# A decoder layer on one core: norms of six experts' weights taken during the recurrence, from staged copies

## The reference

```python
# 1. over 128 time steps, batch 16: an SSM state of 64 and a GRU state of 128
h_ssm = silu(h_ssm @ A.T + bxt);  r, z = sigmoid(i_r + h_r), sigmoid(i_z + h_z)
n = tanh(i_n + r * h_n);  h_rnn = (1 - z) * n + z * h_rnn
fused = g0 * (h_ssm @ Cw.T + Cb + dxt) + g1 * (h_rnn @ proj_w.T + proj_b)
# 2. retention over the context (per batch entry, decay mask, xpos)
out = ((q @ k.T) * mask) @ v
# 3. mixture of experts: 8 experts, top 2 of 8, capacity 320 tokens each
h = relu(xin @ w1[e] + b1[e]);  out = h @ w2[e] + b2[e]      # w1 256x1024, w2 1024x256
```

## Time and profile before

| what | value |
|---|---|
| runs without a profile | 504.99, 505.45, 508.36 us (median 505.45) |
| the profiled execution | 511.01 us, of which 509.2 us is the span of its instructions |
| busy share of the span | PE 80%, DVE 75%, ACT 46%, POOL 27% |
| granted TensorE clock, mean | 0.899 of full |
| HBM read, written | 35.04 MB, 11.01 MB |

### The profile page before, as it was taken

One profiled execution on the slowest core, in us unless ns is written; L12 is line 12 of the kernel. 1 busy time (PEld: TensorE's weight loads), 2 busy tenths in 40 slices (PEclk: granted clock), 3 DMA queues, 4 the chain that ended last, 5 costly groups with the idle time before them and its releaser, 6 DMA issues.

```text
span 509.2 us, 13431 instructions
## 1 busy us (share of the span) xinstructions
PE 405.5 (80%) x4676; PEld 312.4 (61%) x4676; DVE 382.2 (75%) x1575; ACT 235.2 (46%) x802; POOL 138.6 (27%) x207
## 2 busy tenths in 40 slices
PE   3979889899998999999999676217999999998000
PEld 3535667687786878778777565214677777776000
DVE  4477878987869879797867837686798888894184
ACT  0455265433233333333323224323988888963053
POOL 0013323211212112131201311044135554313384
PEclk9989989999799999999959789556999999999655
DMA  7970119020110201111011000006435656101482
GB/s 249 307 254 1 33 32 321 13 63 3 32 51 1 81 0 37 45 31 51 0 35 41 23 1 21 24 11 210 151 122 167 211 201 204 43 13 48 130 290 103
DMA packets 38238, 46.49 MB, mean 91 GB/s; under 512 B 4283, under 2 KB 32702, under 8 KB 38202
## 3 DMA queue, kind: packets, MB, share of 16 engines
q1 hardware_dynamic: 35002, 36.62, 22.2%
q0 software_dynamic: 3200, 9.40, 5.8%
HBM read 35.04 MB, written 11.01 MB: 90 GB/s over the span
## 4 chain that ended last, share of the span: by engine, by line
PE 45%; DVE 28%; issue 10%; ACT 9%; DMA 4%; POOL 3%; SPq 0%; ACTq 0%; DVEq 0%; POOLq 0%
PE bank L756 43%; DVE h L1123 3%; DVE mb L1114 3%; DVE ub L1112 3%; ACT arena L674 2%; DVE h L1126 2%; DVE hist L1124 2%; DMA wbuf<-in_w 2%; ACT arena L665 1%; DVE st L1186 1%; DVE vp L1460 1%; DVE tm L1155 1%; DVE mb L1115 1%; PE bank L1037 1%; ACT rzb L550 1%
## 5 line engine op out<-in xcount | busy, mean ns | idle before, releaser
L550 ACT ACTIVATE rzb<-bank 128x32 f32<-128x32 f32 x128 | 25.4, 198 | 99.3 <-PE bank L756 98.2
L756 PE MATMUL bank<-h,whp 128*128 128x32 f16 x1152 | 62.8, 185 | 5.1 <-DVE h L1123 2.6
L1112 DVE TENSOR_TENSOR_SCAN ub<-rzb,bank 128x32 f32<-128x32 f32 x128 | 27.9, 218 | 50.1 <-ACT rzb L550 49.1
L756 PE MATMUL bank<-arena 128*128 128x320 f16 x384 | 56.0, 304 | 1.4 <-DVE arena L1507 1.4
L756 PE MATMUL bank<-arena,kp 128*128 128x320 f16 x384 | 54.5, 299 | 0.0
L756 PEld LDWEIGHTS bank<-h,whp 128*128 128x128 f16 x1152 | 42.3, 97 | 15.4 <-DVE h L1126 3.5
L553 ACT ACTIVATE nb<-ub 128x16 f32<-128x16 f32 x128 | 27.9, 218 | 47.2 <-DVE ub L1112 47.2
L756 PEld LDWEIGHTS bank<-arena 128*128 128x128 f16 x384 | 37.7, 100 | 16.4 <-DVE arena L1507 1.6
L756 PEld LDWEIGHTS bank<-hsb,at_w 66*64 66x64 f32 x256 | 25.9, 140 | 34.7 <-DVE hsb L1118 22.5
L756 PEld LDWEIGHTS bank<-arena,kp 128*128 128x128 f16 x384 | 37.3, 98 | 14.1
L756 PE MATMUL bank<-hsb,at_w 66*64 66x16 f32 x256 | 37.3, 222 | 7.1 <-DVE hsb L1118 6.9
(11 more groups left out here) (206 smaller groups left out, 936.3 us busy)
## 6 DMA issues: line engine op xcount, KB each, us to landing
wbuf<-in_w SPq DMA_DIRECT2D x16, 1024.0 KB, 6.1
ybuf<-zero POOLq DMA_DIRECT2D x8, 512.0 KB, 7.4
wbuf<-ybuf SPq DMA_DIRECT2D x16, 256.0 KB, 5.6
xin_t<-in_xT SPq DMA_DIRECT2D x16, 128.0 KB, 2.3
arena<-in_ctxT SPq DMA_DIRECT2D x4, 512.0 KB, 7.5
xfin_t<-in_xT SPq DMA_DIRECT2D x16, 128.0 KB, 2.2
xres<-in_xtok SPq DMA_DIRECT2D x16, 128.0 KB, 2.1
x_d<-x SPq DMA_DIRECT2D x8, 256.0 KB, 2.3
```

What stands on the lines that cost most here:

```text
L550: nc.scalar.activation(od(rzb[:]), RZ[j][:, s * 2 * B:(s + 1) * 2 * B], ACT.Sigmoid).then_inc(q["r_ready"], 1)
L756: return nc.tensor.matmul(out_, lhsT, rhs, start=start, stop=stop, skip_group_check=True)
L1112: nc.vector.tensor_tensor_scan(ub[:], rzb[:, 0:2 * B], NS[j][:, s * 32:s * 32 + 32], 0.0, ALU.mult, ALU.add).then_inc(q["npre_ready"], 1)
```

## The change

The scales of all eight experts are made at once, ahead of the expert stage. For experts 2 to 7, iteration g of the recurrence squares expert g: `w1[g]` and `w2[g]` (1 MB each) are loaded to two stages in `arena[0]`, and ACT squares one piece of 128x512 of them after each of the steps 3, 4, 5, 8 (first layer), 9, 10, 12, 15 (second layer), and `b1[g]` after the last. SP asks for the next expert's first layer once ACT has squared the fourth piece, and for its second layer once it has squared the eighth; both requests stand inside `inputs(g)`. Those of expert 2 are asked for together in `inputs(1)`. Experts 0 and 1 are squared from `wbuf` as before. One matmul of 80 columns, one reduction, one power (16 elements per partition on POOL) and one set of scales serve all experts; `norms` and `scales` leave the expert loops of PE, DVE and POOL, and `squares` that of ACT. The weights are loaded a second time for the expert stage as before, so 12 MB are read twice. The diff, cut to its core (declarations, the changes of indices and the end of `squares` are left out):

```diff
+SQ_STEP = (3, 4, 5, 8, 9, 10, 12, 15)
+SQ_N = 5
...
+        b1s = sb("b1s", [P, E * FK])
+        wsum2 = sb("wsum2", [P, 2, E, SQ_N])
...
+        stage = [view(arena[0], 0, 4, 512), view(arena[0], 2048, 4, 512)]
+        wjunk = [arena3[:, 1536:2048].bitcast(BF16), arena3[:, 1024:1536].bitcast(BF16)]
...
+            def stage_1(g):
+                sp.dma_start(stage[0].rearrange("p a b -> p (a b)").rearrange("p (h f) -> p h f", h=HD), w1_d[:, g]).then_inc(q["wst0"], 16)
+
+            def stage_2(g):
+                sp.dma_start(stage[1].rearrange("p a b -> p (a b)").rearrange("p (k d) -> p k d", k=FK), w2_d[:, g]).then_inc(q["wst1"], 16)
+
             def inputs(g):
                 load_in(2 * g + 2, 0)
+                if not isinstance(g, int):
+                    sp.wait_ge(q["stq_ready"], 9 * (g - 2) + 5)
+                    stage_1(g + 1)
+                elif g == 1:
+                    sp.wait_ge(q["v_mm"], B)
+                    sp.wait_ge(q["csqs"], HD * B)
+                    stage_1(2)
+                    stage_2(2)
                 load_fin(2 * g + 2, 0)
+                if not isinstance(g, int):
+                    sp.wait_ge(q["stq_ready"], 9 * (g - 2) + 9)
+                    stage_2(g + 1)
                 load_in(2 * g + 3, 1)
                 load_fin(2 * g + 3, 1)
...
-            def norms(e):
-                pool.wait_ge(q["wnrm_ready"], 2 * e + 2)
-                pool.tensor_tensor(winv[e % 2][:], wnrm[e % 2][:], mhalf[:, 0:2], ALU.pow).then_inc(q["winv_ready"], 1)
-
-            norms(0)
+            pool.wait_ge(q["wnrm_ready"], 2)
+            pool.tensor_tensor(winv[:], wnrm[:], mhalf[:], ALU.pow).then_inc(q["winv_ready"], 1)
...
-                if e + 1 < E:
-                    norms(e + 1)
...
+            def stage_square(g, p):
+
+                if p % 4 == 0:
+                    act.wait_ge(q[f"wst{p // 4}"], 16 * (g - 1))
+                act.wait_ge(q["stq_ready"], 9 * (g - 2) + max(p, 1))
+                nc.scalar.activation(wjunk[p % 2][:, 0:512], stage[p // 4][:, p % 4, :], ACT.Square,
+                                     accum_out=wsum2[:, p // 4, bass.ds(g, 1), p % 4]).then_inc(q["stq_ready"], 1)
+                if p == 7:
+                    act.wait_ge(q["stq_ready"], 9 * (g - 2) + 8)
+                    nc.scalar.activation(wjunk[0][:, 0:FK], b1t[:, bass.ds(g * FK, FK)], ACT.Square,
+                                         accum_out=wsum2[:, 0, bass.ds(g, 1), 4]).then_inc(q["stq_ready"], 1)
+
             def iteration(g, A, M):
                 for s in range(CH):
                     rec(g, s // ST, s % ST)
+                    if M and s in SQ_STEP:
+                        stage_square(g, SQ_STEP.index(s))
...
+            def w_high(e, j, p, i):
+                if p % 2 == 0:
+                    act.wait_ge(q[f"w{p // 2 + 1}l{j}"], 16 * i + 16)
                 nc.scalar.activation(quarter(w1p[j][0], w2p[j][0], p), quarter(w1t[j], w2t[j], p), ACT.Copy,
-                                     scale=wscl[j][:, p // 2:p // 2 + 1]).then_inc(q["w_hi"], 1)
+                                     scale=wscl[:, bass.ds(p // 2 * E + e, 1)]).then_inc(q["w_hi"], 1)
...
+            squares(0)
             exponentials(1, TILES - 4, TILES)
-            squares(1, 1, 0)
+            squares(1)
+            act.wait_ge(q["wscl_ready"], 4)
...
-                if not (isinstance(e, int) and e >= E - 2):
-                    squares(e + 2, j, i + 1)
...
-            def norms(e, j, bk=1):
-                pe.wait_ge(q["wsq_ready"], 5 * e + 5)
-                mm(bank[bk][:, 384:390], ones[:], wsum2[j][:].rearrange("p w k -> p (w k)")).then_inc(q["wnsum"], 1)
-
-            norms(0, 0, 6)
+            pe.wait_ge(q["wsq_ready"], 10)
+            mm(bank[6][:, 384:384 + 2 * E * SQ_N], ones[:], wsum2[:].rearrange("p w e k -> p (w e k)")).then_inc(q["wnsum"], 1)
...
-                if not (isinstance(e, int) and e == 0):
-                    pe.wait_ge(q["wnrm_ready"], 2 * e + 1)
...
-                    if f == 1 and not last_:
-                        if not (first or isinstance(e, int) and e < 2):
-                            pe.wait_ge(q["yt_ready"], 2 * e - 2)
-                        norms(e + 1, 1 - j)
...
+            def norms():
+                dve.wait_ge(q["wnsum"], 1)
+                nc.vector.tensor_reduce(wtot[:], bank[6][:, 384:384 + 2 * E * SQ_N].rearrange("p (n k) -> p n k", k=SQ_N),
+                                        AX.X, ALU.add).then_inc(q["wnrm_ready"], 1)
+                dve.wait_ge(q["wnrm_ready"], 1)
+                nc.vector.tensor_scalar(wnrm[:], wtot[:], TINY, None, ALU.max).then_inc(q["wnrm_ready"], 1)
+
+            def scales():
+                dve.wait_ge(q["winv_ready"], 1)
+                nc.vector.tensor_scalar(wscl[:], winv[:], W_UP, None, ALU.mult).then_inc(q["wscl_ready"], 1)
+                dve.wait_ge(q["wscl_ready"], 1)
+                nc.vector.tensor_tensor(b1s[:].rearrange("p (e f) -> p e f", e=E), b1t[:].rearrange("p (e f) -> p e f", e=E),
+                                        wscl[:, 0:E].unsqueeze(2).to_broadcast([P, E, FK]), ALU.mult).then_inc(q["wscl_ready"], 1)
+                nc.vector.tensor_tensor(wprod[:], wscl[:, 0:E], wscl[:, E:2 * E], ALU.mult).then_inc(q["wscl_ready"], 1)
+                dve.wait_ge(q["wscl_ready"], 3)
+                nc.vector.reciprocal(wund[:], wprod[:]).then_inc(q["wscl_ready"], 1)
...
-                    if f == 1 and not last:
-                        norms(e + 1, 1 - j)
...
-                    if f == 4 and not last:
-                        scales(e + 1, 1 - j)
```

More of the change, by code:

```diff
@@ L112, in mk_decoder_kernel @@
         ones = sb("ones", [P, P])
-        mhalf = sb("mhalf", [P, 4])
+        mhalf = sb("mhalf", [P, 2 * E])
         epst = sb("epst", [P, 2])
@@ L215, in mk_decoder_kernel @@
         w2p = [[w[:, HD * FF:].rearrange("p (k d) -> p k d", k=FK) for w in ws] for ws in wparts]
[L216 to L225, removed]
+        b1s = sb("b1s", [P, E * FK])
+        wsum2 = sb("wsum2", [P, 2, E, SQ_N])
+        wtot = sb("wtot", [P, 2 * E])
+        wnrm = sb("wnrm", [P, 2 * E])
+        winv = sb("winv", [P, 2 * E])
+        wscl = sb("wscl", [P, 2 * E])
+        wprod = sb("wprod", [P, E])
+        wund = sb("wund", [P, E])
+        stage = [view(arena[0], 0, 4, 512), view(arena[0], 2048, 4, 512)]
+        wjunk = [arena3[:, 1536:2048].bitcast(BF16), arena3[:, 1024:1536].bitcast(BF16)]
         hp = [arena[0][:, i * FK * CAP // 2:(i + 1) * FK * CAP // 2].bitcast(F16).rearrange("p (f c) -> p f c", f=FK) for i in range(2)]
@@ L462, in _ @@
             pool.wait_ge(q["nrm_done"], 1)
[L463 removed]
+            pool.tensor_tensor(inv[:], nrm[:], mhalf[:, 0:4], ALU.pow).then_inc(q["inv_done"], 1)
             iteration(1, True, False)
@@ L656, in _, with squares @@
             x1T_copy(CHUNKS - 1)
-            def squares(e, j, i):
+            def squares(e):
+                act.wait_ge(q["stq_ready"], 9 * (CHUNKS - 2) + 1)
                 for p in range(4):
                     if p % 2 == 0:
[L661 to L664, removed]
+                        act.wait_ge(q[f"w{p // 2 + 1}l{e}"], 16)
+                    src = quarter(w1t[e], w2t[e], p)
+                    if 5 * e + p > 1:
+                        act.wait_ge(q["wsq_ready"], 5 * e + p - 1 if p > 1 else 5 * e)
                     nc.scalar.activation(wjunk[p % 2].rearrange("p (a b) -> p a b", a=src.shape[1]), src, ACT.Square,
-                                         accum_out=wsum2[j][:, p // 2, p % 2:p % 2 + 1]).then_inc(q["wsq_ready"], 1)
+                                         accum_out=wsum2[:, p // 2, e, p % 2:p % 2 + 1]).then_inc(q["wsq_ready"], 1)
                 act.wait_ge(q["wsq_ready"], 5 * e + 3)
[L668 to L673, removed]
+                nc.scalar.activation(wjunk[0][:, 0:FK], b1t[:, e * FK:(e + 1) * FK], ACT.Square,
+                                     accum_out=wsum2[:, 0, e, 4:5]).then_inc(q["wsq_ready"], 1)
+            def w_high(e, j, p, i):
+                if p % 2 == 0:
+                    act.wait_ge(q[f"w{p // 2 + 1}l{j}"], 16 * i + 16)
                 nc.scalar.activation(quarter(w1p[j][0], w2p[j][0], p), quarter(w1t[j], w2t[j], p), ACT.Copy,
-                                     scale=wscl[j][:, p // 2:p // 2 + 1]).then_inc(q["w_hi"], 1)
+                                     scale=wscl[:, bass.ds(p // 2 * E + e, 1)]).then_inc(q["w_hi"], 1)
             def exponentials(part, a, b):
@@ L713, in expert @@
                     if f >= 6 and not last:
-                        w_high(e + 1, 1 - j, f - 6)
+                        w_high(e + 1, 1 - j, f - 6, i + j)
                 if not last:
-                    w_high(e + 1, 1 - j, 2)
-                    w_high(e + 1, 1 - j, 3)
-                if not (isinstance(e, int) and e >= E - 2):
-                    squares(e + 2, j, i + 1)
+                    w_high(e + 1, 1 - j, 2, i + j)
```

(16 more changed lines are left out.)

20 lines of the change are left out of this document (2 added, 18 removed).

## The result

The changed kernel takes 520.55 us (518.83 to 521.83), the kernel before 505.22 in the same session: ratio 1.0279, 95% interval 1.0249 to 1.031, that is 12.6 to 15.7 us slower (the ratio goes by the fast executions alone; the two medians would give 1.0303). The forecast was 511.7 and the range ended at 518. The profiled execution took 518.83 us, span 517.0, mean granted clock 0.889 where it was 0.899.

A forecast was written before the change was run, and what follows sets the result against it. PE was taken as full in both recurrence and experts. 7.0 + 0.3 + 1.4 - 4.0 = 4.7 us lost, plus 1.7 for one more clock drop, on 505.45 gave 511.85, said as 511.7; range 503.0 to 518.0.

The forecast's parts named there:

- Experts, 4.0 gained: Expert loop: PE no longer makes the next expert's norm between blocks 1 and 2; 4.0 us gained, bounds 3.1 to 4.5.
- One power, 1.4 lost: POOL before the first gather: a 16-element power takes 2.9 us, delaying the gather 1.4 us; bounds 0.5 to 2.3.
- Squares, 0.3 lost: Recurrence: ACT's squares fit gaps before the sigmoids, costing 0.05 us in each of six iterations; bounds 0 and 7.
- Nothing held up: Rival at `in_a`, iterations 3 to 7: the small load isn't held up; 2.3 us gained, 503.2 us, chance 0.13.
- The requests in SP's queue, 7.0 lost: Small load behind the 1 MB request makes PE wait 1.4 us at `in_a`, iterations 3 to 7; bounds 5.0 to 10.5.
- I take one more drop ... 1.7: PE in iterations 3 to 7: one more half-clock stretch, 3.1 us less 1.4 of waiting it hides, 1.7 lost.
- Clock: Rival: each wait at `in_a` brings PE down to 1.2 GHz for a stretch, five at 3.1 us; 518.7 us, chance 0.13.
- The squares aren't hidden: Rival in the recurrence: squares delay the sigmoids by 0.15 us each, 7 us more than taken; 518.5 us, chance 0.07.
- The profile test in the last paragraph: Signs in the profile of a right or wrong prediction; more or fewer than two stretches at clock 0.50 meant wrong.

The follow-up runs named there:

- the small load first: Changed kernel with SP issuing the small load that `in_a` needs ahead of the second layer's request; 505.99 us, ratio 0.9969 to the kernel before.
- the wait filled: Changed kernel with three useless float32 matmuls on PE just before the wait in `in_a`, iterations 3 to 7; 512.98 us, ratio 1.0137 to the kernel before.
- the tiny squares: Changed kernel with each staged square reading 8 columns instead of 512, loads and order unchanged; 520.81 us, ratio 1.0269 to the kernel before.
- the large load alone: Kernel before plus one 1 MB load, read by nobody, ahead of the small load in iterations 2 to 6; 523.56 us, ratio 1.0295.
- the one with half of it: Kernel before plus one 0.5 MB load, read by nobody, ahead of the small load in iterations 2 to 6; 512.06 us, ratio 1.0123.
- without stage loads: Changed kernel with only expert 2 staged, later squares reading the same data again; 505.41 us, ratio 0.9968 to the kernel before.
- the power split either way: Small load issued first, power in two parts: the second before expert 1's gather (504.11 us, ratio 0.9964) or behind it (503.25 us, 0.9943).
- the filler without the wait: The same three useless PE matmuls in the kernel with the small load first; 512.66 us, ratio 1.0122 to the kernel before.
- the queue of its own: Changed kernel with the loop's second-layer request issued from ACT's queue behind the last piece's square; 515.75 us, ratio 1.0187 to the kernel before.

## Why the prediction was wrong

- **Experts, 4.0 gained: right.** Before to after, the start of expert 1 is 11.76 us late and that of expert 7 is 7.71 late: 4.05 gained, with 14.5 us per expert.
- **One power, 1.4 lost: right.** 2.90 us long as worked out, 1.36 lost. Not foreseen: the first five blocks' matmuls of expert 0 then ran some 0.8 us longer, at 1.2 GHz.
- **Squares, 0.3 lost: nearly right.** With the small load first an iteration takes 30.69 us instead of 30.57, so 6 x 0.12 = 0.7.
- **Nothing held up: the rival's size.** I gave 503.2, that is 2.3 gained, for a small load that isn't late. The small load first is this case: 1.6 gained (0.6 to 2.5).
- **The requests in SP's queue, 7.0 lost: the mechanism right, the size too small.** The wait is where the prediction put it, in the same five iterations. Listed it is 1.56 + 1.38 + 2.47 + 1.42 + 2.85 = 9.7 us, within the bounds of 5.0 to 10.5. On the time it costs 1.68%, 8.5 us: the ratio with the wait filled less the one with the small load first. Three of the five are the 1.4 us of the forecast (its own rows give 201.67 - 200.18 = 1.5). The surplus stands in iterations 5 and 7, whose small loads landed after 6.3 and 6.6 us where the others took 5.2 to 5.4. In iteration 7 this comes back in other runs (6.3 with the tiny squares, 6.2 with the large load alone), in iteration 5 it doesn't (5.4); why is open.
- **"I take one more drop ... 1.7": the step that failed.** The clock's part is the changed kernel less the one with the wait filled, 1.42%, 7.2 us (each interval is 1.5 to 2 us wide on either side). In the profiled iterations this difference is 168.1 - 162.3 = 5.9, of which 4.5 is the slower clock and 1.4 that the data came earlier after the issue with the wait filled. So the clock cost 4.5 us in the fastest execution and up to 7.2 by the times, where 1.7 was taken. The ratio puts the changed kernel at 1.0279 x 505.45 = 519.6, 7.7 over the sum of 511.85: 5.5 by the clock, 1.5 by the wait and 0.7 by the rest. Had the clock taken only its 1.7, this would be 514.1, inside the range. The rival called *Clock* had the mechanism and gave 518.7, of a measured 520.55. I argued against it that "most iterations show none". But the iterations that I counted had no wait in them, so they said nothing of iterations that do. The two drops with "little idle PE before them" were the evidence that bore on it: PE's gaps in those iterations are at most 0.53 us, and each of the five waits is 2.6 times that or more.
- The sum given for the rival *The squares aren't hidden*, 518.5, is 511.85 + 7 = 518.9 by its own terms; nothing hangs on it.
- The profile test in the last paragraph did its work: "PE's clock at 0.50 for more ... stretches than two" was named as a sign that the prediction is wrong.

What stays open is the exact condition for a drop. Counted over the stretches from copy to copy of all the profiled executions: of 16 waits for the small load of 1.30 us or more, 14 have a drop at them (four of five in the changed kernel and with the tiny squares, all five with the large load alone, the one with half of it). In the runs with the small load first, without stage loads and with the power split either way, 0 of 20 iterations have one; with the wait filled 0 of 5. But the kernel before has 2 in 5, the filler without the wait 1 in 5, and the queue of its own 3 in 5, after gaps of 0.4 to 0.5 us at the end of an iteration, of which a fourth brought none. So a long wait makes a drop likely and is not needed for one; what tips it otherwise the runs don't tell.

## What to carry to other kernels

When a bulk transfer is added, look for the next small load behind it that an engine without slack needs soon: asking for that one first made 2.8% of loss into 0.3% of gain, with the same bytes. Giving the bulk transfer another queue didn't bring the small load sooner; only the order in time did. And here a wait on an engine whose clock already falls now and then cost one and a half to nearly two times its length (9.7 us of waiting and 4.5 of clock in the profile, 8.5 and 7.2 by the times), so price it so, or put work into it. A slow instruction that serves many consumers at once (here a power of 16 elements) can be cut so that the first consumer waits only for its part, if the rest goes behind everything urgent in that queue.

## What the hardware showed that I had not expected

- A load of 128 KB asked for 0.57 us after one of 1 MB lands 5.2 to 6.6 us after its issue, where 2.1 to 2.5 is its own; from another queue and 1.35 us after it, 5.2 to 5.6. Behind 0.5 MB it took 3.7 to 5.1.
- TensorE fell to 1.2 GHz for 3.4 to 10.2 us at four of the five waits of 1.4 to 2.9 us in the changed kernel, in iterations in which it was otherwise busy for 29 of 31 us. The page on TensorE in the Trainium skill (TensorE: Matmul & The Clock Gate, A second HAM failure mode: psum-queue depth-cycling) tells of a kernel whose short idle spells between groups of matmuls make the clock swing between its levels. The drops of the kernel before, of the filler without the wait and of the queue of its own agree with it: no gap of PE in those iterations is over 0.53 us. Those at the waits are of another kind, each at one idle spell of 1.4 us or more.
- POOL's power grows by about 0.156 us for each further element per partition: 0.551 us for one element, 1.019 for four, 2.31 to 2.50 for twelve, 2.90 for sixteen.
